# A post-norm cross-attention layer on one core: z and q through DRAM, z turned in 32x32 blocks by VectorE

## The reference

```python
q, k, v = heads(x @ Wq + bq), heads(ctx @ Wk + bk), heads(ctx @ Wv + bv)
scores = q @ k.T / sqrt(16); scores = where(j < i, scores, -1e30)
attn = softmax(scores); attn[:, :, 0, :] = 0
x = layer_norm(x + merge(attn @ v) @ Wo + bo, ln1_g, ln1_b)
out = layer_norm(x + relu(x @ W1 + b1) @ W2 + b2, ln2_g, ln2_b)
```

## Time and profile before

| | |
|---|---|
| median of the runs | 1664.52 us |
| the profiled execution: its time, its span | 1664.95 us, 1663.1 us |
| PE, ACT, DVE, POOL busy | 1622.1 (98%), 1545.7 (93%), 1434.9 (86%), 1379.0 (83%) |
| granted TensorE clock, mean | 0.985 |
| DMA | 208.99 MB, mean 126 GB/s |
| chain that ended last | PE 95%, DVE 2%, ACT 1%, issue 1%, DMA 1% |

### The profile page before, as it was taken

One profiled execution on the slowest core, in us unless ns is written; L12 is line 12 of the kernel. 1 busy time (PEld: TensorE's weight loads), 2 busy tenths in 40 slices (PEclk: granted clock), 3 DMA queues, 4 the chain that ended last, 5 costly groups with the idle time before them and its releaser, 6 DMA issues.

```text
span 1663.1 us, 54091 instructions
## 1 busy us (share of the span) xinstructions
PE 1622.1 (98%) x16700; PEld 1595.2 (96%) x16700; DVE 1434.9 (86%) x6744; ACT 1545.7 (93%) x5907; POOL 1379.0 (83%) x1352
## 2 busy tenths in 40 slices
PE   4799999999999999999999999999999999999997
PEld 4799999999999999999999999999999999999997
DVE  3688898898898898898898898898898898898885
ACT  3799999999999999999999999999999999999993
POOL 2378888888888888888888888888888888888896
PEclk7799999999999999999999999999999999999999
DMA  8856656656656655656665666655666666765530
GB/s 152 168 120 124 130 134 122 131 126 128 132 135 119 133 133 119 133 133 119 135 136 115 136 131 119 135 134 118 134 135 119 132 133 121 132 135 121 120 69 27
DMA packets 307087, 208.99 MB, mean 126 GB/s; under 512 B 164336, under 2 KB 281968, under 8 KB 306800
## 3 DMA queue, kind: packets, MB, share of 16 engines
q1 hardware_dynamic: 305104, 204.60, 59.8%
q10 hardware_dynamic: 1696, 0.92, 0.3%
HBM read 104.73 MB, written 50.33 MB: 93 GB/s over the span
## 4 chain that ended last, share of the span: by engine, by line
PE 95%; DVE 2%; ACT 1%; SPq 1%; DMA 1%; issue 1%; POOL 0%; POOLq 0%; ACTq 0%; DVEq 0%
PE ps_dense L386 32%; PE ps_dense L397 32%; PE ps_probsT L493 14%; PE ps_scores L483 7%; PE ps_att L511 7%; PE ps_dense L368 2%; ACT probs L588 0%; DVE ps_scores L795 0%; PE ps_att L410 0%; DMA probs<-in_L_xattn_Wk_dram 0%; DMA q_stack<-qT 0%; SPq L240 0%; SPq L246 0%; SPq L262 0%; SPq L283 0%
## 5 line engine op out<-in xcount | busy, mean ns | idle before, releaser
L588 ACT ACTIVATE probs<-ps_scores,negmax 128x128 f32<-128x128 f32 x2048 | 741.7, 411 | 8.6 <-DVE negmax L795 5.1
L1046 POOL TENSOR_TENSOR probs<-probs,recip 128x512 f32<-128x512 f32 x512 | 530.9, 1037 | 136.6 <-DVE recip L778 136.5
L795 DVE CUSTOM_DVE_ANT_0 ps_scores<-ps_scores,mask 128x128 f32<-128x128 f32 x2048 | 527.1, 318 | 71.6 <-PE ps_scores L483 69.3
L588 ACT ACTIVATION_READ_ACCUMULATOR probs<-ps_scores,negmax 128x1 f32 x2048 | 515.4, 252 | 0.0
L397 PE MATMUL ps_dense<-w,hT 128*128 128x256 f32 x3048 | 418.0, 286 | 0.9 <-DVE u L920 0.9
L386 PE MATMUL ps_dense<-zT,w 128*128 128x256 f32 x3072 | 416.9, 285 | 0.8 <-DVE h_f L879 0.5
L1054 POOL TENSOR_TENSOR hT<-h_f,hT 128x512 fp32r<-128x512 f32 x252 | 321.2, 1284 | 90.3 <-DVE h_f L879 90.3
L386 PEld LDWEIGHTS ps_dense<-zT,w 128*128 128x128 f32 x3072 | 381.8, 189 | 1.5 <-issue 0.9
L397 PEld LDWEIGHTS ps_dense<-w,hT 128*128 128x128 f32 x3048 | 377.5, 188 | 1.2 <-DVE u L920 1.1
L605 ACT ACTIVATE probsT<-ps_probsT 128x508 f32<-128x508 f32 x512 | 318.7, 623 | 39.5 <-PE ps_probsT L493 39.5
L493 PE MATMUL ps_probsT<-ident,probs 128*128 128x128 f32 x2048 | 313.8, 275 | 0.0
(11 more groups left out here) (92 smaller groups left out, 2350.1 us busy)
## 6 DMA issues: line engine op xcount, KB each, us to landing
k_stack<-k_spill SPq DMA_DIRECT2D x384, 128.0 KB, 4.4
q_stack<-qT SPq DMA_DIRECT2D x762, 64.0 KB, 2.0
k_spill<-kT SPq DMA_DIRECT2D x128, 256.0 KB, 2.2
c_tok<-in_ctx_dram SPq DMA_DIRECT2D x256, 64.0 KB, 4.8
x_res<-in_x_dram SPq DMA_DIRECT2D x64, 256.0 KB, 3.2
x_tok<-in_x_dram SPq DMA_DIRECT2D x252, 64.0 KB, 2.4
out_dram<-o_tok SPq DMA_DIRECT2D x63, 256.0 KB, 2.7
probsT<-in_L_xattn_W_dram SPq DMA_DIRECT2D x1, 1024.0 KB, 11.0
```

The source lines that it names most:

```text
L588: last = nc.scalar.activation(probs[:, m % 4, i, :], ps_scores[m % 2][:, i, :], ACT.Exp, bias=negmax[:, m % 4, i:i + 1], scale=-1.0, accum ...
L795: last = nc.vector.tensor_tensor_reduce(ps_scores[m % 2][:, i, :], ps_scores[m % 2][:, i, :], mask[:], -1.0, -MASKED, ALU.add, ALU.min, ac ...
L1046: nc.gpsimd.tensor_tensor(probs[:, m % 4], probs[:, m % 4], recip[:, m % 4, :].unsqueeze(2).broadcast_to([P, 4, S]), ALU.mult)\
```

## The change

z is stored to DRAM from `u1` (`spill_z`), read back in 32x32 blocks over the residual's tile `x_res` (`load_z`), turned in place by one DVE transpose (`z_flips`) and split from there (`z_hi`, `z_lo`). PE's `z_transpose` and the bank zT go. The next residual is loaded into `x_res` after `z_lo`. q of all groups but the first is stored to DRAM in two DMAs (`spill_q`) and loaded in three (`stack_q`); its product is made three groups ahead instead of two. Down-projection runs one round later against the scores than before. The lists of all five engines and the table of banks are new. In the prologue the product v of group 0 and the splits of Wv and Wo stand ahead of the loop; W1's rows and the two columns that are folded into it are loaded by block. The last group's second norm is computed for each sequence as (u - mean) * gain and then * rstd + offset, two `scalar_tensor_tensor`, without ACT; its two stores leave from SP and ACT.

The core of the diff:

```diff
-ITERATIONS = range(-5, NG + 6)
-
-BANK = {"zT": 2, "v": 0, "q": 2, "f1_0": 2, "k": 0, "f1_1": 1, "f1_2": 2, "f1_3": 0, "wo": 1, "f2": 1}
-
-HELD_BY = {"zT": ("q", -3), "f1_0": ("zT", 0), "f1_2": ("f1_0", 0), "q": ("f1_2", 4), "k": ("v", 2),
-        "f1_3": ("k", -3), "v": ("f1_3", 2), "f1_1": ("f2", 1), "wo": ("f1_1", 1), "f2": ("wo", -1)}
+ITERATIONS = range(-7, NG + 6)
+
+BANK = {"v": 2, "q": 1, "f1_0": 2, "k": 2, "f1_1": 1, "f1_2": 0, "f1_3": 2, "wo": 2, "f2": 0}
+
+HELD_BY = {"f1_3": ("v", -2), "k": ("f1_3", 4), "f1_0": ("k", -3), "wo": ("f1_0", 1), "v": ("wo", 1),
+        "f1_1": ("q", -4), "q": ("f1_1", 5), "f2": ("f1_2", 0), "f1_2": ("f2", 1)}
...
+        z_dram = nc.dram_tensor("z_spill", (2, GB, S, D), F32).ap()
+        z_blocks = z_dram.rearrange("g b (o t) (j n) -> g j t (b o) n", t=32, j=4)
...
+        q_dram = nc.dram_tensor("q_spill", (2, 2, KC, P, GT), F32).ap()
+        q_rows = q_dram.rearrange("n h c (j r) t -> n h r (c j) t", j=4)
...
-        q_stack = [sb(f"q_stack{i}", [PARTS * 32, 4, KC, GT], F32R) for i in range(2)]
+        q_stack = [sb(f"q_stack{i}", [PARTS * 32, 4 * KC, GT], F32R) for i in range(2)]
...
+        z_tile = x_res[:].rearrange("p b d -> p (b d)").rearrange("p (o k) -> p o k", k=KC * 32)
+
+        def z_by_chunk():
+            return z_tile.rearrange("p o (c t) -> p c o t", c=KC)
+
+        q_by_pair = q_stack[0][:].rearrange("p (c j) t -> p j c t", j=4)
...
+            def spill_q(g, part):
+                if exists(g) and g > 0:
+                    if part == 0:
+                        sp.wait_ge(s_hi["q"], KC * (g + 1))
+                    else:
+                        sp.wait_ge(taken["q"], KC * (g + 1))
+                    need(sp, s_qstack, 16 * PARTS * (g - 2))
+                    sp.dma_start(q_dram[g % 2, part].rearrange("c p t -> p c t"), f32(qT[:, part])).then_inc(s_qspill[part], 16)
+
+            def stack_q(g, part):
+                if exists(g) and g > 0:
+                    sp.wait_ge(s_qspill[part], 16 * g)
                     need(sp, s_scores, (g - 1) * UNITS)
                     for s, half in enumerate(QPART):
-                        for j in (2 * i, 2 * i + 1):
-                            sp.dma_start(f32(q_stack[g % 2][32 * s:32 * s + 32, j]),
-                                         f32(qT[32 * j:32 * j + 32, half])).then_inc(s_qstack[i], 16)
+                        if half == part:
+                            sp.dma_start(f32(q_stack[g % 2][32 * s:32 * s + 32]), q_rows[g % 2, part]).then_inc(s_qstack, 16)
...
-                    need(sp, taken["wo"], g)
+                    need(sp, s_zlo, g)
                     sp.dma_start(x_res[:], x_v[g]).then_inc(s_xres, 16)
+
+            def spill_z(g):
+                if exists(g):
+                    sp.wait_ge(s_z1, GB * (g + 1))
+                    need(sp, s_zrow, 16 * 4 * (g - 1))
+                    sp.dma_start(z_dram[g % 2].rearrange("b s d -> s b d"), u1[:]).then_inc(s_zspill, 16)
+
+            def load_z(g):
+                if exists(g):
+                    sp.wait_ge(s_zspill, 16 * (g + 1))
+                    sp.wait_ge(taken["wo"], g + 1)
+                    for j in range(4):
+                        sp.dma_start(z_tile[32 * j:32 * j + 32], z_blocks[g % 2, j]).then_inc(s_zrow, 16)
...
             def iteration(it):
-                stack_k(it + 2, 0)
-                next_c(it + 4)
-                stack_q(it + 3, 0)
+                spill_k(it + 3, 0)
+                stack_q(it + 3, 1)
                 load_residual(it + 1)
-                stack_q(it + 3, 1)
-                spill_k(it + 3, 0)
                 spill_k(it + 3, 1)
+                stack_k(it + 3, 0)
+                stack_k(it + 3, 1)
                 store(it - 2)
-                next_x(it + 5)
-                stack_k(it + 3, 1)
+                spill_q(it + 4, 0)
+                next_c(it + 5)
+                spill_z(it + 1)
+                spill_q(it + 4, 1)
+                stack_q(it + 4, 0)
+                load_z(it + 1)
+                next_x(it + 7)
 
             load_c(0)
             load_weight(1)
             for dram, tile in COLS:
                 sp.dma_start(tile[:], dram.rearrange("(c p) -> p c", p=P), allow_slow_non_contiguous=True).then_inc(s_wc, 16)
+            load_weight(2)
+            load_weight(3)
+            sp.dma_start(bv_row[:], bv.rearrange("(a n) -> a n", a=1).broadcast_to([P, D])).then_inc(s_bv, 16)
             load_x(1)
             load_c(1)
             spill_k(0, 0, True)
             stack_k(0, 0, True)
             stack_k(0, 1, True)
             load_x(2)
-            stack_q(0, 1, True)
+            stack_q0(2)
+            stack_q0(3)
             load_c(2)
-            load_weight(2)
-            load_weight(3)
-            for dram, tile in ROWS:
+            for dram, tile in ROWS[1:]:
                 sp.dma_start(tile, dram.rearrange("(a n) -> a n", a=1).broadcast_to([P, D])).then_inc(s_wr, 16)
             load_weight(4)
+            for dram, tile in BLOCK_COLS:
+                by_block = dram.rearrange("(j c d) -> j d c", j=4, c=KC)
+                for j in range(4):
+                    sp.dma_start(tile[32 * j:32 * j + 32], by_block[j], allow_slow_non_contiguous=True).then_inc(s_wb, 16)
+            load_weight(5)
...
-            def z_transpose(g):
-                if exists(g):
-                    pe.wait_ge(s_z1, GB * (g + 1))
-                    transposes(g, "zT", u1)
...
             def iteration(it):
                 scores(it, 0)
-                probs_transpose(it - 1, 4)
-                z_transpose(it - 2)
-                ff_down(it - 3, 2)
+                ff_up(it - 3, 3)
+                probs_transpose(it - 1, 5)
                 scores(it, 1)
-                probs_transpose(it - 1, 5)
-                ff_down(it - 3, 3)
-                ff_up(it - 2, 0)
+                ff_down(it - 3, 0)
+                probs_transpose(it - 1, 6)
+                ff_down(it - 3, 1)
                 scores(it, 2)
-                probs_transpose(it - 1, 6)
+                probs_transpose(it - 1, 7)
                 k_project(it + 1)
                 scores(it, 3)
-                ff_up(it - 2, 1)
-                probs_transpose(it - 1, 7)
-                ff_up(it - 2, 2)
+                probs_transpose(it, 0)
+                ff_down(it - 3, 2)
                 scores(it, 4)
                 attend(it - 1)
-                probs_transpose(it, 0)
-                ff_up(it - 2, 3)
+                probs_transpose(it, 1)
+                ff_down(it - 3, 3)
                 scores(it, 5)
-                probs_transpose(it, 1)
+                ff_up(it - 2, 0)
+                probs_transpose(it, 2)
+                scores(it, 6)
+                ff_up(it - 2, 1)
+                probs_transpose(it, 3)
                 out_project(it - 1)
-                scores(it, 6)
-                probs_transpose(it, 2)
-                q_project(it + 2)
+                scores(it, 7)
+                ff_up(it - 2, 2)
                 v_project(it)
-                ff_down(it - 2, 0)
-                scores(it, 7)
-                probs_transpose(it, 3)
-                ff_down(it - 2, 1)
+                probs_transpose(it, 4)
+                q_project(it + 3)
...
-                    take_hi("zT", zT, g, full["f1_3"], g)
+                    act.wait_ge(s_zflip, g + 1)
+                    need(act, full["f1_3"], g)
+                    nc.scalar.activation(zT[:, 0].rearrange("p c (o t) -> p c o t", t=32), z_by_chunk(), ACT.Copy)\
+                      .then_inc(s_hi["zT"], 1)
...
+            def z_flips(g):
+                if exists(g):
+                    dve.wait_ge(s_zrow, 16 * 4 * (g + 1))
+                    nc.vector.transpose(z_tile, z_tile).then_inc(s_zflip, 1)
+
             def z_lo(g):
                 if exists(g):
-                    take_lo("zT", zT, g)
+                    dve.wait_ge(s_hi["zT"], g + 1)
+                    nc.vector.tensor_tensor(zT[:, 1].rearrange("p c (o t) -> p c o t", t=32), z_by_chunk(),
+                                            f32(zT[:, 0]).rearrange("p c (o t) -> p c o t", t=32), ALU.subtract)\
+                      .then_inc(s_zlo, 1)
...
+                    dve.wait_ge(s_lsum, b + 1)
+                    nc.vector.bn_stats(stats[:, 1, b, :], u2[:, b, :]).then_inc(s_lst, 1)
+                    dve.wait_ge(s_lst, b + 1)
+                    nc.vector.bn_aggr(mv[:, 1, b, :], stats[:, 1, b, :]).then_inc(s_lmv, 1)
+                    dve.wait_ge(s_lmv, b + 1)
+                    nc.vector.tensor_scalar(var_eps[:, 1, b:b + 1], mv[:, 1, b, 1:2], LN_EPS, None, ALU.add).then_inc(s_lve, 1)
+                    nc.vector.tensor_scalar(neg_mean[:, 1, b:b + 1], mv[:, 1, b, 0:1], -1.0, None, ALU.mult).then_inc(s_lnm, 1)
+                    dve.wait_ge(s_lnm, b + 1)
+                    nc.vector.scalar_tensor_tensor(out=u2[:, b, :], in0=u2[:, b, :], scalar=neg_mean[:, 1, b:b + 1],
```

(5 more changed lines are left out.)

279 lines of the change are left out of this document (144 added, 135 removed).

## The result

The changed kernel takes **1683.14 us** (median of 4 runs, 1681.73 to 1684.82) against 1664.47 for the kernel before (4 runs): a ratio of 1.0113, 95% interval 1.0100 to 1.0125. It is slower by 1.1%, where I had forecast 0.5% faster, and it lies outside the range of 1643 to 1678. The profiled execution has a span of 1679.9 us (before 1663.1) at a mean granted clock of 0.977 (before 0.985).

The account below looks back on a forecast made before the run. The prediction took PE, busy 200 of 200 us, as the bound. Passes -25, start +13.8 and end +3 summed to -8.2 us on the span of 1663.1, giving a median of about 1656 us, range 1643 to 1678.

Parts of the forecast that it names:

- The pass term: Steady loop: PE without z's transposes makes a pass 24.45 us instead of 24.86, -25 us over sixty-one passes.
- my bounds of -21 and -36: Limits of the steady-pass saving: only z's own 0.35 us gives -21; none of the added cost for scores gives -36.
- The start term: Prologue: x 3 loads late, first maximum 19.3 us later, less 1.5 and 4 regained behind it: +13.8 us.
- the upper bound that I had named: Start: first maximum 23 us later if x 3 lands 6 us after issue, as behind large loads.
- The end term: Last group: z's trip poorly hidden, +5 us, and the last norm as two DVE operations, -2: +3 us.
- Rival 1: Slower by z's round trip through DRAM: PE waits 0.4 us per pass, +24 on the sum, 1680 us; chance 0.15.
- Rival 2: Slower or level by ACT still idling 0.86 us per pass: passes of 24.96, 1687 us at worst; chance 0.17.
- Rival 3: Start hidden: if x 3 arrives by 38 us, the start costs 2 instead of 13.8: 1644 us; chance 0.12.
- Rival 4: z's transposes on PE are worth their durations, 256 x 273 ns, -70 instead of -25: 1611 us; chance 0.03.

Follow-up runs that it names:

- run 3: Changed kernel with scores 1 and scores 6 moved one place ahead on PE, so none stand right behind transposes: 1682.49 us, ratio 1.0097.
- run 16: Changed kernel with prologue in first-use order, first scores earlier, last z on PE, and second norm's moments behind the fourth take of h on DVE: 1661.09 us, ratio 0.9978.
- run 2: Changed kernel without z's round trip: z neither stored nor loaded back, DVE turns what the residual's tile holds: 1678.15 us, ratio 1.0076.
- run 5: Kernel before the change with one of z's four transposes per group instead of four: 1644.86 us, ratio 0.9874.

## Why the prediction was wrong

**The pass term (-25 us, measured -14.9) failed in its second half.** Its first part holds: z's transposes cost 0.35 us by the starts. The rest of the sum does not. By the starts of 16 passes, in us per pass:

| blocks | forecast | before | after | measured |
|---|---|---|---|---|
| z's transposes | -0.35 | 0.355 | 0 | -0.355 |
| eight sets of probability transposes | -0.08 | 2.99 | 2.97 | -0.02 |
| twelve dense blocks | -0.16 | 17.63 | 17.62 | -0.01 |
| eight pairs of scores | +0.18 | 2.01 | 2.18 | +0.17 |

Two parts of it failed. The dense blocks: eight came right after transposes before (1.500 on average) and six do after (1.500), which is what I had counted. But I gave all others one price, 1.43. In fact the other four took 1.407 before, since three of them came after dense blocks (1.42, 1.42, 1.37), and the other six take 1.436 after, where five come after scores. Six blocks at 0.03 more make 0.17, and it eats the -0.16 whole. Single blocks after scores take 1.42 to 1.45 in the changed kernel; what decides between these was not found. The scores' +0.18 was real, and run 3 shows that it can't be had back by reordering. The transposes: the 0.08 of extra time ahead of z was gone, and came back ahead of k as a wait for a bank, which run 16 removed. Sum -0.22, and 24.634 - 24.867 = -0.23. The measured -14.9 lies outside my bounds of -21 and -36: the lower one took z's own 0.35 alone, and so let cheaper blocks pay for the scores' +0.18, which they didn't. The place from which I took 0.36 for transposes without z has no wait behind it, and I didn't ask what the moved k would wait for.

**The start term (+13.8) is +22.4.** The way was right (x 3 late on SP, the first maximum behind it, nothing hidden), the sizes were not. The first maximum is 22.7 us later, not 19.3: x 3 was issued from 47.75 rather than 46.5, and its four issues and the landing took 6.8 us, where I had 4.4. That is almost the upper bound that I had named (6 us of landing, a first maximum 23 us late) and not taken. From there to the third group's scores I forecast 1.5 less than before, 47.9, and it is 52.1. PE is as busy in this stretch as before (36.57 us and 36.28) and idle 2.5 us longer; it waits mostly for ACT in both, and no run takes this part by itself. The third pass gave 3.0 back, not 4.

**The end term (+3) is +9.2, and a part of it is missing from the sum.** I took 4 us off the start because the third pass has fewer blocks of the two feed-forward products, and put nothing in the end, where as many come back: 32 dense blocks where 29 stood, PE busy 4.4 us longer. The term that I did count came out smaller: the trip of z took 9.1 us from the norm where I had 8.1, but four blocks of down-projection (6 us), and not the 3 us of before, cover it, so that z costs a gap of 2.40 us (2.6 by run 2) and not 5. Instead PE waits 2.2 us in the end for POOL's h (1.66 once), where it waited for none, and 1.5 for v. The last norm gives back about 1.2, not 2.

**The rivals.** Rival 1, z's trip, which I held for the likeliest mechanism on the slow side together with ACT: refuted by the run without the trip. The Trainium skill's rule on transfers under 512 B (DMA: Bandwidth & Descriptors, Specifications) spoke for it; z's loads land in 3.9 us, between x's 2.4 and c's 4.8, and no pass is longer for it. Rival 2, ACT: refuted by a pass of 24.56 with ACT's work of before (run 5) and one of 24.57 with that of the change (run 16). Rival 3, a hidden start: refuted, x 3 came at 54.5 where it needed 38. Rival 4: refuted by the single transpose. The time landed on the slow side by none of the named rivals: all three terms of my sum missed in the same direction, by 10, 9 and 6 us. No bound that I had named covers them: -21 for the passes, and for the start a first maximum 23 us late, which makes 17.5 in place of 13.8. Even with both, and 3 for the end, it would have been about level, 0.5 us less.

What I said would show the forecast wrong did so in part: a pass of 24.63 is longer than 24.6, yet with neither DVE's turn of z waiting in it nor PE waiting for ACT. I had no case in which PE stays full and the gain is simply smaller.

## What to carry to other kernels

On a saturated engine, price a reordering by a table of (block before, block, block after) over the whole pass, old and new, and check that a cost removed from one block doesn't reappear on another. When work moves to a later round, what the start saves the end pays: count the blocks behind the same point in both kernels. A change that needs one more group of lead pays for it in the prologue: write down that queue's list with the landing times under load, since whatever stands last there moves the whole run, and fixing one wait uncovers the next until the list is in the order of first use. Here that order and the first scores ahead of later projections were worth some 20 us, more than the change gains in all its passes.

## What the runs showed that I had not expected

A small operation of DVE can last until one of POOL's ends. Timeline of POOL and DVE in the changed kernel:

```profile
798.64 1.04 POOL L1107 TENSOR_TENSOR probs<-probs,recip 128x512 f32<-128x512 f32 x1 [0.19 <-DVE recip L833]
...
798.80 0.90 DVE L959 TENSOR_SCALAR var_eps<-mv 128x2 f32<-128x2 f32 x1
```

and in run 16, where the same addition falls at the end of the same operation:

```profile
803.60 1.04 POOL L1152 TENSOR_TENSOR probs<-probs,recip 128x512 f32<-128x512 f32 x1 [0.74 <-DVE recip L870]
...
804.49 0.17 DVE L1001 TENSOR_SCALAR var_eps<-mv 128x2 f32<-128x2 f32 x1
```

128x2 elements take 0.90 us in the first and 0.17 in the second, and both end within 0.03 us of POOL's end (799.68, 804.64). z's subtraction, at 808.33 for 1.27 us, ends 0.55 us after POOL's operation of 807.77 to 809.05. For z's subtraction this fits the Trainium skill (SBUF — State Buffer, SBUF: two separate sides), by which DVE and POOL share a pair of ports as an exclusive lock, for a DVE operation with two inputs in SBUF or in a 2-port performance mode. The addition has one such input; whether it runs in such a mode no run here shows, and none tried POOL's side. It cost no time that can be told, as PE stayed full. It would also explain why z's subtraction takes more than the 0.81 that I had read from c's: c's at 800.64, with no operation of POOL beside it, takes 0.71. That was read from the rows and not tried.
